# Reordering the pairs of query tiles in a differential attention block, on one Trainium2 core

## The chip, the cores and the metric

The kernel runs on one core of one Trainium2 chip. The metric is the device time of one execution in microseconds, taken as the median of several runs; lower is better.

## What is computed

The input is one sequence of 2048 tokens with 256 channels. Cut to what matters here:

```python
qkv = hidden_states @ Wqkv_w.T + Wqkv_b          # 16 query heads, 8 key heads, D = 128
p1 = softmax(causal(q[..., 0] @ k[..., 0].T * scale))
p2 = softmax(causal(q[..., 1] @ k[..., 1].T * scale))
p = p1 - lam * p2
o = p @ v                                        # v has 2 * D = 256 columns a head
o = o * rsqrt(mean(o * o) + EPS) * subln_w * (1 - LAMBDA_INIT)
x = x + layernorm(o @ out_w.T + out_b)           # attention block
x = x + layernorm(ffn(layernorm(x)))             # feed-forward block, 256 -> 1024 -> 256
```

The attention is differential: each of 8 output heads has two softmax maps, which are combined before the product with the values. It is causal, so a query tile of 128 tokens with number i has (i + 1) * 128 keys, 128 for tile 0 and 2048 for tile 15. Everything is in float32, and TensorE gets each operand as a high and a low part of float32r.

## The kernel before, in words

After a prologue that normalises and transposes the input, the attention is a hardware loop of 4 iterations (`nc.Fori(0, GROUPS)`), one for each group of key heads, with all semaphores cleared at its end (`all_engine_barrier`, line 930). A feed-forward stage follows; it reads the results of all tiles and does not depend on the order in which they were made.

A group serves two output heads, s = 0 and s = 1, so there are 2 x 16 rows of work: a **row** is one query tile of one head, with its two maps m = 0 and m = 1. `duo_chunks` puts two rows in a **duo**: tile 15 - e of head 0 and tile e of head 1, the shorter first. A duo has always 17 key blocks of 128, cut in 5 **chunks** of at most 512 keys. Two duos (e even and the next e) are a **pair**, since their queries are projected together (`QP`), and `PAIR_ORDER` says in which order the 8 pairs come. Pair p and pair 7 - p have the same row lengths: 0 and 7 hold tiles 0, 15, 1, 14 (rows of 1 and 4 chunks), 1 and 6 tiles 2, 13, 3, 12, 2 and 5 tiles 4, 11, 5, 10, and 3 and 4 tiles 6, 9, 7, 8 (rows of 2 and 3 chunks).

`attention_steps` turns this into one list of steps, and every engine walks through the same list in order, waiting on semaphores. It is made in **halves** h, one for each map of each duo (32 halves, and 3 more that drain the pipeline); half h holds the scores of duo h // 2, map h % 2. The strings `FIRST_HALVES`, `HALVES` and `LAST_HALVES` give the interleaving within a half. The kinds of step:

- `S` (line 583, matmuls of lines 596 to 598): scores of one chunk, three matmuls in one of 4 score banks. The bank of the chunk 4 before must have been read by its exponential on ScalarE (`score_bank`, line 532). VectorE reduces each chunk to its maximum (line 801; line 796 for a row's last chunk, with the causal mask), and after a row's last chunk makes the row's negated maximum (line 805). Only then can ScalarE take the exponentials of all chunks of that row (line 702): their places in its queue are set by `exps_due` and `EXPS_AT`.
- factors: when the second map of a row has its exponentials, VectorE sums (line 865) and GpSimd makes the ratio (lines 882, 885). Then each chunk is mixed, e1 + ratio * e2: chunk 3 of a duo on VectorE (line 873), the others on GpSimd (lines 895, 898).
- `T` (line 605): transposes of a mixed chunk; ScalarE copies the high part (line 713), VectorE the low part (line 811).
- `PV` (lines 618, 620): product with the values, two matmuls a key block. After a row's last chunk ScalarE copies one half (line 722) and VectorE adds (line 822), which gives o_sum.
- `OT` (line 649) transposes o_sum, lines 729 and 828 split it, and `OP` (line 659) is the output projection, added into acc by VectorE (line 856).
- `K`, `V`, `W` and the first `QP` are projections and transposes at the head of an iteration.

The products of duo d are due three to four halves after its scores: half 3 and half 4 hold those of duo 0.

```python
EXPS_AT = {'PV': 2, 'OT': 0, 'QP': 0, 'T': 0, 'S': 2, 'OP': 2}
HALVES = ('TSSTSSPTSoQTPPPTO', 'TSTSSOSTPSoQTPPTP')
FIRST_HALVES = ('KQSKKKSVSVSSVVVVV', 'SVWSWSQSS')
LAST_HALVES = ('ToTPTToOP', 'TTOTPPTPO', 'ToTTTOoPo')
SCALAR_LAGS = {'K': 1, 'V': 1, 'QP': 0, 'OP': 0}
VECTOR_LAGS = {'PV': 1, 'T': 1, 'OT': 1, 'W': 1, 'K': 1, 'V': 1}
```

In these strings `P` takes the next `PV`, `o` the next `OT` if a row is finished, and `O` the next `OP` if one is transposed. A lag puts an engine's part of a step behind the next step's.

Of the kernel before, what the change touches and what calls it, by code (L numbers as in the profile page):

```python
# [51 lines left out]
V_USES = TILES // 2  # L52


PAIR_ORDER = (3, 7, 4, 2, 5, 1, 6, 0)


HALVES = ('TSSTSSPTSoQTPPPTO', 'TSTSSOSTPSoQTPPTP')
# [19 lines left out]
def duo_chunks(d):  # L78
# [3 lines left out]
    out = []  # L82
    e = 2 * PAIR_ORDER[d // 2] + d % 2
    for n, (i, s) in enumerate(sorted(((TILES - 1 - e, 0), (e, 1)))):
# [94 lines left out]
def build(nc, hidden, wqkv, bqkv, lq1, lk1, lq2, lk2, subln, out_w, out_b, su_ug, su_dp, ws_ug, ws_dp,  # L179
# [7 lines left out]
    with ExitStack() as whole:  # L187
# [25 lines left out]
        with ExitStack() as att:  # L213
# [271 lines left out]
            def first_q_token(u, s):  # L485
                first = 2 * PAIR_ORDER[u]
                return (TILES - 2 - first) * P if s == 0 else first * P
# [1007 lines left out]
```

## Time and profile before

| | us |
|---|---|
| runs (3) | 1506.24, 1507.68, 1508.19 |
| median | 1507.68 |
| span of the profiled execution, first to last instruction | 1506.7 |
| attention iterations, first weight transpose to the next one's | 23.6, 347.0, 670.2, 991.9 (starts) |

For the profiled execution only its span was given, no time of its own; the median of the runs is 1.0 us above that span. In the iteration that starts at 347.0 us the first scores begin at 363.2, the scores of the second pair at 402.2, the last score chunk ends at 639.9, and the last output projection ends at 665.2. The other iterations look alike. Durations in the trace: a matmul's own time includes its drain through the array, so matmuls overlap and what one costs is the distance from its start to the next one's; "idle before" counts only what is left outside.

### The profile page before, as it was taken

Reading aid. Unit: us, or ns where it says so; the run is one execution under the profiler, and the core shown is the slowest. Engines: PE = TensorE matmul, PEld = TensorE weight load, DVE = VectorE, ACT = ScalarE, POOL = GpSimd, SP = SyncE. Lnnn points to the kernel's source line nnn. Section 1 sums busy time; section 2 is a strip of 40 time slices with the busy share of each in tenths; the row PEclk is TensorE's granted clock in tenths of the full one; section 3 lists DMA queues with packets and bytes.
Section 4 is the critical chain, followed back from the end, with each engine's and each line's share of the span. In section 5 each row is a group of like instructions: output and inputs, shape, how many; then the busy total and the mean of one; then the engine's idle time right before and its main releaser. Section 6 shows DMA issues by size and latency. Waiting matters only on the chain. (4 is left out here: it accounts for less than half of the span.)

```text
span 1506.7 us, 26747 instructions
## 1 busy us (share of the span) xinstructions
PE 1404.5 (93%) x8440; PEld 1228.7 (82%) x8440; DVE 1058.8 (70%) x2630; ACT 881.2 (58%) x2489; POOL 829.8 (55%) x1316
## 2 busy tenths in 40 slices
PE   5999999988999999979999999979999999669998
PEld 4888888877888888867888888768888888547887
DVE  6677777754777787846777887647777777585654
ACT  4566666653666667645667666536666666353331
POOL 1566665650766666634666656607656566433544
PEclk9999999998999999999999999989999999979999
DMA  4000000001000000010000000010000000130000
GB/s 144 8 2 1 1 2 1 1 2 45 8 1 1 1 1 1 1 41 12 2 1 1 1 1 1 1 45 8 1 1 1 2 1 1 17 124 1 11 15 32
DMA packets 25569, 20.46 MB, mean 14 GB/s; under 512 B 8896, under 2 KB 24128, under 8 KB 25408
## 3 DMA queue, kind: packets, MB, share of 16 engines
q1 hardware_dynamic: 25408, 18.52, 4.1%
q8 instruction: 76, 1.25, 0.3%
q14 instruction: 85, 0.70, 0.1%
HBM read 16.41 MB, written 2.10 MB: 12 GB/s over the span
## 5 line engine op out<-in xcount | busy, mean ns | idle before, releaser
L702 ACT ACTIVATE e<-score_bank,negmx 128x512 f32<-128x512 f32 (+3 forms) x640 | 393.8, 625 | 78.8 <-DVE negmx L805 78.2
L898 POOL TENSOR_TENSOR e<-e 128x512 f32<-128x512 f32 (+3 forms) x256 | 284.2, 1110 | 21.4
L618 PE MATMUL turn_bank<-v_hl,pT_hi 128*128 128x512 f32 x784 | 288.4, 403 | 7.8 <-DVE pT_lo L811 7.4
L801 DVE TENSOR_REDUCE mx<-score_bank 128x1 f32<-128x512 f32 x384 | 261.2, 682 | 29.7 <-PE score_bank L598 28.8
L596 PE MATMUL score_bank<-k_hi,q_hi 128*128 128x512 f32 (+3 forms) x640 | 257.5, 402 | 10.4 <-ACT e L702 9.7
L882 POOL TENSOR_TENSOR inv_s<-s,neg_one 128x1 f32<-128x1 f32 x128 | 70.3, 549 | 309.2 <-DVE s L865 309.2
L598 PE MATMUL score_bank<-k_hi,q_lo 128*128 128x512 f32 (+3 forms) x640 | 235.7, 368 | 0.0
L597 PE MATMUL score_bank<-k_lo,q_hi 128*128 128x512 f32 (+3 forms) x640 | 235.3, 368 | 0.0
L620 PE MATMUL turn_bank<-v_hl,pT_lo 128*128 128x256 f32 x784 | 219.8, 280 | 0.0
L895 POOL TENSOR_SCALAR e<-e,ratio 128x512 f32<-128x512 f32 (+3 forms) x256 | 177.8, 694 | 12.2
L618 PEld LDWEIGHTS turn_bank<-v_hl,pT_hi 128*128 128x128 f32 x784 | 147.2, 188 | 41.3 <-DVE pT_lo L811 12.2
L796 DVE CUSTOM_DVE_ANT_0 score_bank<-score_bank,mask 128x256 f32<-128x256 f32 (+3 forms) x256 | 126.0, 492 | 54.2 <-PE score_bank L598 53.3
L620 PEld LDWEIGHTS turn_bank<-v_hl,pT_lo 128*128 128x128 f32 x784 | 148.3, 189 | 2.3
L596 PEld LDWEIGHTS score_bank<-k_hi,q_hi 128*128 128x128 f32 x640 | 121.8, 190 | 30.5 <-ACT e L702 16.8
L598 PEld LDWEIGHTS score_bank<-k_hi,q_lo 128*128 128x128 f32 x640 | 121.7, 190 | 20.1
L702 ACT ACTIVATION_READ_ACCUMULATOR e<-score_bank,negmx 128x1 f32 x640 | 131.9, 206 | 0.0
L597 PEld LDWEIGHTS score_bank<-k_lo,q_hi 128*128 128x128 f32 x640 | 122.6, 192 | 6.5
L922 POOL TENSOR_TENSOR v_hl<-e,v_hl 128x512 fp32r<-128x512 f32 x32 | 41.0, 1296 | 137.4 <-ACT v_hl L743 137.4
L713 ACT ACTIVATE pT_hi<-turn_bank 128x512 fp32r<-128x512 f32 (+2 forms) x124 | 69.7, 562 | 49.5 <-PE turn_bank L605 49.3
L811 DVE TENSOR_TENSOR pT_lo<-turn_bank,pT_hi 128x512 fp32r<-128x512 f32 (+2 forms) x124 | 78.1, 630 | 5.8 <-ACT pT_hi L713 5.2
L1461 POOL TENSOR_TENSOR h_lo<-h_f,h_hi 128x512 fp32r<-128x512 f32 x32 | 41.6, 1299 | 68.3 <-ACT h_hi L1358 68.3
L713 ACT ACTIVATE pT_hi<-sum_bank 128x512 fp32r<-128x512 f32 (+3 forms) x100 | 54.9, 549 | 40.5 <-PE sum_bank L605 39.9
(299 smaller groups left out, 3560.2 us busy)
## 6 DMA issues: line engine op xcount, KB each, us to landing
w_raw<-in_L_attn_Wqkv_w_dram SPq DMA_DIRECT2D x5, 512.0 KB, 3.5
w_raw<-in_L_attn_Wqkv_w_dram SPq DMA_DIRECT2D x10, 256.0 KB, 3.7
x_in<-_attn_hidden_states_dram SPq DMA_DIRECT2D x4, 512.0 KB, 5.7
e<-in_L_attn_out_w_dram SPq DMA_DIRECT2D x4, 512.0 KB, 4.3
out_dram<-d_out SPq DMA_DIRECT2D x16, 128.0 KB, 1.7
x_res<-_attn_hidden_states_dram SPq DMA_DIRECT2D x1, 1536.0 KB, 11.9
bv<-in_L_attn_Wqkv_b_dram SPq DMA_DIRECT2D x10, 128.0 KB, 4.1
raw<-in_L_ffn_W_up_dram SPq DMA_DIRECT2D x2, 512.0 KB, 6.2
```

The costliest lines, as they stand in the source:

```text
L596: pe.matmul(bank[:, 0:w], qh, kh, start=True, stop=False)
L597: pe.matmul(bank[:, 0:w], qh, kl, start=False, stop=False)
L598: pe.matmul(bank[:, 0:w], ql, kh, start=False, stop=True).then_inc(s_full, 1)
L618: pe.matmul(bank[:, :], pT_hi[:, q % PT_SLOTS, b * P:(b + 1) * P], v_hl[:, kt, :], start=(kt == 0), stop=False)
L620: mm = pe.matmul(bank[:, 0:HID], pT_lo[:, q % PT_SLOTS, b * P:(b + 1) * P], v_hl[:, kt, 0:HID], start=False, stop=(kt == i))
L702: act.activation(e, S[k % NS][:, 0:w], ACT.Exp, bias=negmx[:, d % 2, m, s:s + 1], accum_out=ssum[:, d % 4, s, m, c:c + 1]).then_inc(s_act, 1)
L713: act.activation(pT_hi[:, q % PT_SLOTS, 0:w], bank_for(kind, what)[:, 0:w], ACT.Copy).then_inc(t_hi, 1)
L796: dve.tensor_tensor_reduce(out=S[k % NS][:, 0:w], in0=S[k % NS][:, 0:w], in1=mask[:, BANK - w:], scale=1.0, scalar=LOWEST, op0=ALU.add, op ...
L801: dve.tensor_reduce(mx[:, d % 2, m, s, c:c + 1], S[k % NS][:, 0:w], X, ALU.max)\
L811: dve.tensor_tensor(pT_lo[:, q % PT_SLOTS, 0:w], bank_for(kind, what)[:, 0:w], pT_hi[:, q % PT_SLOTS, 0:w].bitcast(F32), ALU.subtract)\
L895: pool.tensor_scalar(b, b, ratio[:, d % 4, s:s + 1], 0.0, ALU.mult, ALU.add)\
L898: pool.tensor_tensor(a, a, b, ALU.add).then_inc(p_pool, 1)
```

## The change

The order of the pairs is changed, and nothing else. Since `duo_chunks`, `first_q_token` and `attention_steps` all read it, the lengths of rows and chunks move to other places in the list of steps, and with them the places of exponentials, factors and mixes.

```diff
-PAIR_ORDER = (3, 7, 4, 2, 5, 1, 6, 0)
+PAIR_ORDER = (0, 7, 1, 6, 2, 5, 3, 4)
```

Widths of the chunks, shorter row | longer row, in the four duos at the ends of the list:

| duo | before | after |
|---|---|---|
| 0 | 512 384 \| 512 512 256 | 128 \| 512 512 512 512 |
| 1 | 512 512 \| 512 512 128 | 256 \| 512 512 512 384 |
| 14 | 128 \| 512 512 512 512 | 512 512 \| 512 512 128 |
| 15 | 256 \| 512 512 512 384 | 512 384 \| 512 512 256 |

## Rows read from the trace of the kernel before

**Rows 1.** The page: TensorE busy, and two groups with mean ns.
```profile
PE 1404.5 (93%) x8440; PEld 1228.7 (82%) x8440; DVE 1058.8 (70%) x2630; ACT 881.2 (58%) x2489; POOL 829.8 (55%) x1316
...
L713 ACT ACTIVATE pT_hi<-turn_bank 128x512 fp32r<-128x512 f32 (+2 forms) x124 | 69.7, 562 | 49.5 <-PE turn_bank L605 49.3
L811 DVE TENSOR_TENSOR pT_lo<-turn_bank,pT_hi 128x512 fp32r<-128x512 f32 (+2 forms) x124 | 78.1, 630 | 5.8 <-ACT pT_hi L713 5.2
```

**Rows 2.** One iteration by stretch: PE, PEld, DVE, ACT, POOL busy; granted clock.
```profile
386.40:402.30 15.90, 13.55 (x68) 11.08 (x68) 11.56 (x32) 9.53 (x28) 10.89 (x16) 0.89 0.02 6
402.30:609.70 207.40, 206.91 (x1306) 184.27 (x1305) 159.90 (x408) 139.29 (x420) 131.16 (x217) 1.00 0.00 1
609.70:639.90 30.20, 29.75 (x179) 25.41 (x178) 24.11 (x59) 19.72 (x62) 18.98 (x31) 1.00 0.01 2
639.90:665.20 25.30, 20.30 (x132) 17.49 (x130) 11.51 (x28) 11.08 (x34) 13.20 (x26) 1.00 0.00 1
```

**Rows 3.** What TensorE waited for, 386.5 to 402.3: us, times, longest.
```profile
PE score_bank L596 <- ACT e L702: 2.3, 2, 2.0
```

**Rows 4.** The timeline at the longest of these waits.
```profile
386.44 0.50 PE L596 MATMUL score_bank<-k_hi,q_hi 128*128 128x512 f32 x1
...
387.85 0.42 DVE L796 CUSTOM_DVE_ANT_0 score_bank<-score_bank,mask 128x256 f32<-128x256 f32 x1
...
388.37 0.16 DVE L805 TENSOR_REDUCE negmx<-mx 128x1 f32<-128x3 f32 x1
...
388.56 0.69 ACT L702 ACTIVATE e<-score_bank,negmx 128x512 f32<-128x512 f32 x1 [1.80 <-DVE negmx L805]
...
389.23 0.68 ACT L702 ACTIVATE e<-score_bank,negmx 128x512 f32<-128x512 f32 x1
...
389.39 0.50 PE L596 MATMUL score_bank<-k_hi,q_hi 128*128 128x512 f32 x1 [1.98 <-ACT e L702]
```

**Rows 5.** TensorE alone, 391 to 402.5 us: starts, one matmul each.
```profile
391.46 0.63 PE L596 MATMUL score_bank<-k_hi,q_hi 128*128 128x512 f32 x1
...
397.69 0.40 PE L596 MATMUL score_bank<-k_hi,q_hi 128*128 128x512 f32 x1
...
398.39 0.39 PE L618 MATMUL sum_bank<-v_hl,pT_hi 128*128 128x512 f32 x1
...
400.06 0.33 PE L550 MATMUL turn_bank<-xT_hi,wq_hi 128*128 128x256 f32 x1
...
400.82 0.40 PE L618 MATMUL sum_bank<-v_hl,pT_hi 128*128 128x512 f32 x1
...
401.89 0.60 PE L605 MATMUL turn_bank<-ident,e 128*128 128x128 f32 x4
402.24 0.36 PE L596 MATMUL score_bank<-k_hi,q_hi 128*128 128x256 f32 x1
```

**Rows 6.** Granted clock at that place, in two iterations.
```profile
390.00:394.00 4.00, 4.00 (x16) 3.39 (x15) 2.66 (x9) 1.91 (x7) 3.40 (x6) 0.57 0.00 0
...
712.00:716.00 4.00, 3.54 (x23) 2.79 (x22) 3.23 (x10) 2.35 (x9) 3.71 (x6) 1.00 0.00 0
```

**Rows 7.** What TensorE waited for, 640 to 665 us.
```profile
PE sum_bank L659 <- DVE oT_lo L828: 1.3, 1, 1.3
PE turn_bank L618 <- DVE pT_lo L811: 1.1, 1, 1.1
PE turn_bank L659 <- DVE oT_lo L828: 1.0, 1, 1.0
PE proj_bank L649 <- DVE o_sum L822: 0.9, 1, 0.9
PE turn_bank L605 <- POOL e L898: 0.6, 1, 0.6
```

**Rows 8.** The timeline of the drain.
```profile
661.16 0.38 ACT L722 ACTIVATE o_half<-turn_bank 128x256 f32<-128x256 f32 x1 [1.65 <-PE turn_bank L620]
...
662.06 0.44 PE L649 MATMUL proj_bank<-ident,o_sum 128*128 128x128 f32 x2 [0.93 <-DVE o_sum L822]
```

## The prediction, made before the change was run

> **What bounds the kernel now.** First the busy times of the page: TensorE is busy for 93% of the span [rows 1]. Such a share says little by stages, so next one iteration of the loop by stretch. From 402.3 to 609.7 us TensorE is busy for 206.91 of 207.40 us, and in the following 30.2 us for 29.75 [rows 2]: these are the middle six pairs and then the last one, and they pass with next to no idle time. What is lost lies at the two ends: 2.35 of 15.9 us at the head, and 5.0 of 25.3 us after the last scores [rows 2]. Then the chain of waits, for those two places alone. At the head TensorE waits 2.3 us in two places, both for an exponential to free a score bank [rows 3]; in the drain it waits five times, for split transposes, for a row sum and once for a mix [rows 7]. So an order of pairs can cost or bring something in two places, four times each, and the 207 us between them follow TensorE's work.
>
> The work doesn't change: the same rows, chunks, masks and projections are issued in another order, so every engine's instructions are the same in kind and number. The feed-forward part and the boundary of the iterations (semaphores, weight loads) neither read the order. The question is only which waits of the ends are hidden. I followed `attention_steps` through both orders by hand for the steps at the ends.
>
> **The middle.** The duos with one short and one four-chunk row are pairs 0, 7, 1 and 6, and all four lie in the two stretches that show about 0.5 us of idle each [rows 2], with 1, 6 and 0 one after the other. In the new order the four lie together. Price 0; bounds 0 and 0.5 us an iteration. There is no idle time there to win.
>
> **The head.** Up to the last score chunk of duo 0 (386.44 in the iteration that I follow) the new order has the same work in the same steps, with projections of V and W between, and I take it as unmoved. Then:
>
> 1. *First wait, +0.8 us.* S(1,0,0) reuses the bank of the chunk four before, S(0,1,1). Before, this was a chunk of a row already exponentiated, so it ran at 386.44, and only S(1,0,1) waited, until 389.39, for the exponential of the longer row's first chunk [rows 4]. In the new order S(0,1,1) is itself the first chunk of the four-chunk row, whose maximum needs S(0,1,4). VectorE's queue ahead of that maximum (W's and QP's low parts, one plain maximum) is the same, so the negated maximum comes at 388.4 again, the exponential ends at 389.2 and S(1,0,0) starts at 389.4: 389.39 less 386.44 is 2.95 us without work, where before one chunk of 0.7 to 0.8 us ran in it and 2.2 were lost.
> 2. *The second row, +0.9.* S(1,1,0) reuses the bank of S(1,0,1), again the first chunk of a long row. From the end of S(1,0,4) the chain is: about 0.25 to VectorE, 0.71 from masked maximum to exponential (387.85 to 388.56), 0.67 for the exponential, 0.15 to TensorE [rows 4], and some 0.2 for the plain maximum still running ahead: 2.0 us. In its cover stand QP, 0.76 (400.06 to 400.82 [rows 5]), and a transpose of one block, 0.1 (0.35 for four, 401.89 to 402.24). That leaves 1.15 against the 0.3 that the second wait has now (2.3 less 2.0 [rows 3, 4]).
> 3. *Mix and copy between exponentials, +0.7.* T(0,1) now is a chunk of the long row, mixed only after four exponentials; I take 0.2 of wait, between 0 and the 0.6 of the like wait in the drain [rows 7]. ScalarE's queue puts T(0,1)'s copy (0.56 [rows 1]) between the second and third exponential of duo 1's long row. Exponentials come every 0.67 us [rows 4] and score chunks need 0.70 each (397.69 to 398.39 [rows 5]), so there is no slack to take a copy in: +0.5 at S(1,1,2), bounds 0 and 0.8.
> 4. *A row of one chunk, +1.7.* This is the largest term. Duo 0 has now a row of 128 keys, whose sum is complete with PV(0,0). The list then has S(1,1,4) and at once OT 0: two steps after its PV, where before OT 0 came ten steps later, and nearly every other OT in both lists has ten or more. In TensorE's queue all stands behind OT 0. What it waits for: after T(0,2), ScalarE's copy (0.56) goes ahead of o_half, and VectorE has, in order, T(0,2)'s low part (0.63 [rows 1]), the masked maximum of S(1,1,4) (0.71 [rows 4]) and o_sum (about 0.45, the second half of the 0.90 from copy to OT [rows 8]). With 0.25 to start and 0.1 to end that is 2.7 us from T(0,2), in which PV(0,0), one key block at 0.35 to 0.4 (1.07 for three), and S(1,1,4), three quarters of 0.70 [rows 5], are done: 1.7. Below, if ScalarE and VectorE are free, it is the bare chain, 0.90 from copy to OT (661.16 to 662.06 [rows 8]) and 0.2 before it, less 0.55: 0.5.
>
> Sum of the head: 0.8 + 0.9 + 0.7 + 1.7 = 4.1 us an iteration; low 1.3 (0.8 and the bare 0.5), high 5.3 (with 0.8 and 0.6 in point 3, and 0.5 for the middle). As a check I put the steps one behind the other: S(2,0,0) comes at about 407.4 instead of 402.24 [rows 5], of which 1.0 is work that moved ahead of it (two more key blocks of PV at 0.35 each, 1.07 for three [rows 5], two of T, one OT).
>
> *The clock.* After the wait, two score chunks take 2.07 us (389.39 to 391.46) where 1.40 is the rate elsewhere [rows 4, 5], and the granted clock of that stretch is 0.57, TensorE at 1.2 GHz for most of it; in the next iteration the same wait leaves it at 1.00 [rows 6], so even now it doesn't always fall. The drain, with five waits up to 1.3 us, stays at 1.00 [rows 2, 7]. The new order keeps the first drop and I price more drops at 0. The Trainium skill ("TensorE: Matmul & The Clock Gate", section "A second HAM failure mode: psum-queue depth-cycling") says that TensorE which idles briefly again and again while it cycles through PSUM banks can switch back and forth between its two clocks; the drain here speaks against it, the head for it. By that rule the sum would be the third rival's below.
>
> **The drain, 0.** The last row before has four chunks, now three; but three key blocks of PV only move ahead of the last scores. The waits one by one, after against before [rows 7]: OT 28 now comes two steps after its last PV (six before), behind two exponentials on ScalarE, and waits 1.3, with 0.3 more at the next PV, where before the PV behind the four exponentials waited 1.1. The mix wait of 0.6 goes, since the last row's mixes start earlier against T(15,2); but PV(15,0) now follows its T with only T(15,1) and OP 28 between, and waits 0.7. OP 29, OT 31 and OP 31 (1.3, 0.9, 1.0) stand as before. 1.3 + 0.3 + 0.7 against 1.1 + 0.6 is +0.6; each wait also costs TensorE some 0.25 outside of the idle count, and against that the shorter last row's softmax frees VectorE and ScalarE earlier. I take 0; bounds -1.7 (both old waits gone) and +1.
>
> **Sum.** 4 iterations x 4.1 = 16.4 us on a span of 1506.7: 1523.1. The median of the runs is 1.0 above that span, so 1524.1.
>
> **The rivals.**
> - *The head costs little, the drain nothing.* If ScalarE's and VectorE's queues are freer at OT 0 than I put them, and points 2 and 3 overlap, the head is 1.3 an iteration: 5.2, or 1513. For it: before, similar tight places never show in the middle; against it: there OTs have ten steps of cover.
> - *Faster.* The drain's two waits that hang on the four-chunk last row (1.1 and 0.6, 1.7 together [rows 7]) vanish with a three-chunk row and even rows. It decides if the head costs under 1.7. With the head at 0.8 (the first point alone) it is -0.9 an iteration, 3.6 in all: 1504. For it: these waits are real and hang on the order. Against: OT 28 moves right behind its PV.
> - *Clock drops in the new waits.* Points 2 and 4 make two more waits above 1 us within 16 us. The one now costs 0.67 for the two chunks shown and up to twice that over its whole stretch, so about 1.2. Two more of them an iteration are +2.4, so 4 x 6.5 = 26, or 1534.
> - *It does nothing.* All head waits fall into time that TensorE makes up later. But it is busy throughout the middle [rows 2], so nothing is made up; what is lost stays lost.
>
> **How the numbers follow.** Forecast (head 4, drain 0) 0.52; cheap head 0.17; clock drops 0.14; faster 0.10; nothing 0.07. A measurement of this kernel can tell about 0.2% (3 us) from no change. Slower takes the forecast, the clock case and most of the cheap head: 0.82; same 0.09; faster 0.09. The range leaves out the faster case and part of the clock case: 1509 (a drain 1 better under the cheap head) to 1533 (head at 5.3 and drain at 1, 4 x 6.3 = 25).
>
> **What would show it.** In the changed trace: the wait at line 596 after each iteration's first duo near 2.8 instead of 2.0, a second one near 1.1; one wait of about 1.7 at line 649 for line 822 at the head, which doesn't exist now; the middle still without idle time; the drain within 1 us of its 25.3 less 1.0 for moved work. The prediction is wrong if OT 0 doesn't wait, if the drain loses its waits without new ones, or if the clock falls more than once in a head.

## The result, and the profile after

The changed kernel takes 1513.2 us (median of 5 runs, 1512.14 to 1515.42), the kernel before 1507.68 (5 runs): a ratio of 1.0046, 95% interval 1.0031 to 1.0062. The two medians alone lie 5.5 us apart, a ratio of 1.0037. It is slower, by some 7 us by the ratio, where 16 were forecast. The span of the profiled execution went from 1506.7 to 1510.9 us.

The second iteration by stretch, as [rows 2]; the columns are the length of the stretch, the busy time and count of TensorE, its weight loads, VectorE, ScalarE and GpSimd, then the granted clock, the DMA share and GB/s:

```profile
362.60:385.50 22.90, 22.90 (x159) 21.06 (x158) 15.00 (x32) 13.15 (x30) 10.68 (x9) 1.00 0.03 7
385.50:406.80 21.30, 15.29 (x79) 12.24 (x77) 13.58 (x34) 12.09 (x37) 11.56 (x19) 0.92 0.02 7
406.80:612.00 205.20, 205.15 (x1298) 182.89 (x1295) 158.95 (x404) 138.00 (x413) 129.12 (x211) 1.00 0.01 1
```

The head, from the end of duo 0's scores to the first scores of the second pair, now takes 21.3 us and has 6.0 us of idle time in it, against 15.9 and 2.35 [rows 2]; some 0.4 of the 21.3 is the end of duo 0's last score chunk, which the stretch before leaves out. The middle is 2.2 us shorter, and its 0.5 us of idle time are gone; 1.4 of the 2.2 are steps that now stand ahead of it. What TensorE waited for in the head, as [rows 3] (total, times, longest):

```profile
PE score_bank L596 <- ACT e L702: 4.3, 3, 2.4
PE turn_bank L649 <- DVE o_sum L822: 1.6, 1, 1.6
```

and from the last score chunk on, which ends at 642.1 (640.5 to 666 us), as [rows 7]:

```profile
PE sum_bank L649 <- DVE o_sum L822: 1.1, 1, 1.1
PE turn_bank L659 <- DVE oT_lo L828: 1.0, 1, 1.0
PE turn_bank L649 <- DVE o_sum L822: 0.9, 1, 0.9
PE proj_bank L659 <- DVE oT_lo L828: 0.8, 1, 0.8
PE turn_bank L618 <- DVE pT_lo L811: 0.5, 1, 0.5
```

The timeline of TensorE in the head, each wait with the start of what comes after it:

```profile
388.47 0.58 PE L596 MATMUL score_bank<-k_hi,q_hi 128*128 128x256 f32 x1 [2.36 <-ACT e L702]
...
395.32 0.38 PE L596 MATMUL score_bank<-k_hi,q_hi 128*128 128x256 f32 x1 [1.29 <-ACT e L702]
...
398.06 0.49 PE L596 MATMUL score_bank<-k_hi,q_hi 128*128 128x512 f32 x1 [0.65 <-ACT e L702]
...
402.61 0.44 PE L649 MATMUL turn_bank<-ident,o_sum 128*128 128x128 f32 x2 [1.59 <-DVE o_sum L822]
```

These are the four waits of the prediction's points 1 to 4, in their places. So the head costs about what was forecast, and what is missing must have been given back elsewhere. To find it I made a count of **lateness**: for every step of an iteration the distance from its first matmul to the next step's, less the distance that this kind and width of step commonly has (the lower fifth of all, such as 0.69 us for an S of 512 keys and 1.39 for a PV of 512). Plain distances and lateness together make up an iteration's scores and products; the plain part is 278.1 us in both kernels. Lateness takes in whatever makes a step come late, a wait or a low clock. Mean of iterations 2 to 4, us:

| steps | before | after | difference |
|---|---|---|---|
| 2 to 24, first duo's scores, K, V, W | 0.1 | 0.25 | +0.15 |
| 25 to 45, the head | 4.8 | 8.95 | +4.2 |
| 46 to 353, the middle | 7.7 | 6.9 | -0.8 |
| 354 to 398, the last pair's scores | 2.9 | 1.45 | -1.4 |
| 399 to 425, the drain | 7.2 | 6.9 | -0.3 |
| from first weight transpose to first scores (all 4) | 15.8 | 15.0 | -0.8 |

The sum is +1.05 us an iteration, 4.2 in four, which is the difference of the spans. The +4.2 of the head would alone have been 16.8: about what was forecast, and 12.6 of it came back in sum in the other rows, 8.8 of that in the middle and the last pair's scores.

### The profile page after: what moved, and what is told of

It reads as the page before. It is cut to its first block and busy times, and to the rows that moved or that the text cites. A ratio compares the mean times of both kernels' runs of the same rounds, so it can differ in the third digit from the quotient of the medians.

```text
span 1510.9 us, 26747 instructions
## 1 busy us (share of the span) xinstructions
PE 1401.7 (93%) x8440; PEld 1228.3 (81%) x8440; DVE 1060.1 (70%) x2630; ACT 884.3 (59%) x2489; POOL 829.1 (55%) x1316
## 3 DMA queue, kind: packets, MB, share of 16 engines
q8 instruction: 76, 1.25, 0.4%
## 5 line engine op out<-in xcount | busy, mean ns | idle before, releaser
L618 PE MATMUL turn_bank<-v_hl,pT_hi 128*128 128x512 f32 x596 | 217.4, 400 | 1.9 <-DVE pT_lo L811 1.9
L895 POOL TENSOR_SCALAR e<-e,ratio 128x512 f32<-128x512 f32 (+3 forms) x256 | 176.4, 689 | 12.6
L620 PE MATMUL turn_bank<-v_hl,pT_lo 128*128 128x256 f32 x596 | 167.1, 280 | 0.0
L796 DVE CUSTOM_DVE_ANT_0 score_bank<-score_bank,mask 128x384 f32<-128x384 f32 (+3 forms) x256 | 125.9, 492 | 52.8 <-PE score_bank L598 52.8
L618 PEld LDWEIGHTS turn_bank<-v_hl,pT_hi 128*128 128x128 f32 x596 | 111.9, 188 | 26.0 <-issue 3.3
L618 PE MATMUL sum_bank<-v_hl,pT_hi 128*128 128x512 f32 x340 | 124.4, 400 | 0.0
L620 PEld LDWEIGHTS turn_bank<-v_hl,pT_lo 128*128 128x128 f32 x596 | 112.7, 189 | 1.9
L713 ACT ACTIVATE pT_hi<-turn_bank 128x512 fp32r<-128x512 f32 (+3 forms) x156 | 81.4, 522 | 40.1 <-PE turn_bank L605 39.5
L620 PE MATMUL sum_bank<-v_hl,pT_lo 128*128 128x256 f32 x340 | 95.2, 280 | 0.0
L811 DVE TENSOR_TENSOR pT_lo<-turn_bank,pT_hi 128x512 fp32r<-128x512 f32 (+3 forms) x156 | 90.2, 578 | 2.3 <-ACT pT_hi L713 2.0
```

What stands on the lines that cost most here:

```text
L618: pe.matmul(bank[:, :], pT_hi[:, q % PT_SLOTS, b * P:(b + 1) * P], v_hl[:, kt, :], start=(kt == 0), stop=False)
L620: mm = pe.matmul(bank[:, 0:HID], pT_lo[:, q % PT_SLOTS, b * P:(b + 1) * P], v_hl[:, kt, 0:HID], start=False, stop=(kt == i))
L796: dve.tensor_tensor_reduce(out=S[k % NS][:, 0:w], in0=S[k % NS][:, 0:w], in1=mask[:, BANK - w:], scale=1.0, scalar=LOWEST, op0=ALU.add, op ...
L811: dve.tensor_tensor(pT_lo[:, q % PT_SLOTS, 0:w], bank_for(kind, what)[:, 0:w], pT_hi[:, q % PT_SLOTS, 0:w].bitcast(F32), ALU.subtract)\
L895: pool.tensor_scalar(b, b, ratio[:, d % 4, s:s + 1], 0.0, ALU.mult, ALU.add)\
```

## The experiments

Each ran beside the kernel before on one chip, in three groups on three chips: after_again, long_ends, even_ends and turn_late; before_again, mix_later, even_turn and even_first4; and the three mixes_behind. Ratios are to the kernel before on the same chip. Traces hold one execution each, so the lateness and the median can differ by a few us; those of even_ends and mix_later are of their fastest runs.

**after_again**, the changed kernel for a second profile, and **before_again**, the kernel before.

> The changed kernel unaltered, for a second profile. In the first pair of traces the scores and products of an iteration took 1.5 to 2.5 us longer after the change, while the stretch from the first weight transpose to the first scores, which the order does not touch, took 14.9, 15.05, 15.3 and 14.95 us instead of 15.8, 16.2, 15.1 and 16.3. Theory A (that part is where the clock happens to stand, not the order): the ratio to the kernel before stays within 1.003 to 1.007, and in this second profile that stretch takes other values, some near 16. Theory B (the order has a lasting effect on it): the four values repeat within 0.2 us.

> The kernel before unaltered, for a second profile. In the first one the stretch from the first weight transpose to the first scores took 15.8, 16.2, 15.1 and 16.3 us, and the first head stall was followed by a fall of the clock in three of four iterations; after the change both profiles have that stretch at 14.9 to 15.5. Theory A (chance of where the clock stands): this profile has other values, with a mean that may be near 15. Theory B (bound to the list of steps): again three or four values near 16.

Measured: 1514.84 us, ratio 1.0051 (1.0037 to 1.0065), and one run of the kernel before at 1509.02. The lateness by steps came back within 0.2 us in every stretch of both. The stretch before the first scores: changed kernel 15.5, 14.85, 15.0, 15.0; kernel before 16.0, 16.2, 15.0, 16.1, the same pattern as in its first profile (15.8, 16.2, 15.1, 16.3). So it isn't chance from run to run, and theory B holds for the kernel before. For the changed kernel neither theory is right as written: single values moved by up to 0.6 us, but none is near 16, and the mean is 15.0 and 15.1. What differs is the clock. Kernel before, iterations 2 to 4, columns as above:

```profile
347.00:363.20 16.20, 15.33 (x77) 13.50 (x78) 7.33 (x12) 7.00 (x12) 0.00 (x0) 0.83 0.23 67
670.20:685.30 15.10, 14.22 (x76) 12.66 (x77) 7.64 (x15) 7.00 (x12) 0.00 (x0) 0.89 0.26 79
991.90:1008.20 16.30, 15.44 (x77) 13.60 (x78) 7.33 (x12) 7.00 (x12) 0.00 (x0) 0.82 0.22 67
```

The changed kernel at the same places:

```profile
347.50:362.60 15.10, 14.18 (x76) 12.62 (x77) 7.33 (x12) 7.00 (x12) 0.00 (x0) 0.89 0.25 72
671.40:686.70 15.30, 14.40 (x76) 12.81 (x77) 7.64 (x15) 7.01 (x12) 0.00 (x0) 0.88 0.25 74
996.30:1011.30 15.00, 14.13 (x77) 12.54 (x78) 7.24 (x12) 6.99 (x12) 0.00 (x0) 0.90 0.25 73
```

In both TensorE has just been idle for over 5 us at the boundary of iterations, and for a while it runs at 1.2 instead of 2.4 GHz; a granted clock of 0.89 over the stretch goes with 15 us, one of 0.83 with 16. In these two profiles the new order got the shorter low-clock phase, but that isn't a property of the order: turn_late below has the same order and took 15.8, 16.2, 15.0 and 15.75 us there, like the kernel before, and mixes_behind_after 16.3, 15.9, 15.8 and 15.4. Nothing in the kernel asks for it.

**long_ends**: the long head with a long end.

```diff
-PAIR_ORDER = (0, 7, 1, 6, 2, 5, 3, 4)
+PAIR_ORDER = (0, 3, 4, 2, 5, 1, 6, 7)
```

> Order (0, 3, 4, 2, 5, 1, 6, 7): the head on long rows as after the change, and a long pair (7, the mirror of 0) at the end. Theory A: head +4.1 an iteration and nothing given back at the end: 1507.7 + 16 = 1524, at least 1520. Theory B (the give-back doesn't come from the end of the list): about 1513, as after the change.

Measured: 1519.6 us, ratio 1.0077 (1.0063 to 1.009). 12 us slower than before, between the theories. Its head has the same 8.95 of lateness as the changed kernel, its middle 7.25, its last pair 2.2 and its drain 7.3: about half of what the middle and the last pair had given back is gone with this end, and so is that of the drain, and the stretch before the first scores took 15 us twice and 16 twice.

**even_ends**: the head of before with an end on even rows.

```diff
-PAIR_ORDER = (3, 7, 4, 2, 5, 1, 6, 0)
+PAIR_ORDER = (3, 7, 0, 1, 6, 2, 5, 4)
```

> Order (3, 7, 0, 1, 6, 2, 5, 4): the head of the kernel before (pairs 3, 7) with an end on even rows (5, 4). Theory A: the long rows at the head cost 4.1 us an iteration, and the end on even rows gives some of it back, about 1.5 us in the last pair and drain and up to 0.9 in the middle. Then this order is 1.5 to 2.5 us an iteration faster than the kernel before, 6 to 10 us: 1498 to 1502, with the head at its 5.0 us over the plain work. Theory B: what was given back hangs on the clock after the boundary or on long pairs standing together, not on the end. Then the time is within 2 us of 1507.7.

Measured: 1501.6 us, ratio 0.9963 (0.9949 to 0.9977), 6 us faster than before. The size is theory A's lower end, but not its place: the last pair still has 2.85 us of lateness and the drain 6.9. What fell is the middle (steps 200 to 299 from 3.1 to 2.3), the head (4.2 in all three iterations, with a granted clock of 1.00) and the stretch before the first scores (15.0 each). So "an end on even rows" is not the cause in the last pair.

**turn_late**: the changed order, with the first OT moved.

```diff
-                if to_turn:
+                if to_turn and h != 3:
```

> The changed order, but the first OT of an iteration is put 13 steps behind its PV instead of 2, all later steps keep their distances. Theory A (the fourth point of the prediction): the wait of 1.6 us at line 649 at the head vanishes and nothing takes its place: 1.75 us an iteration, so 7 us less than the changed kernel, about 1506. Rival: TensorE only runs into the next wait for exponentials sooner, since ScalarE and VectorE are behind at this place: less than 0.6 us an iteration is won, 1511 or more.

Measured: 1508.68 us, ratio 1.0013 (1.0004 to 1.0022), 6.2 us less than the changed kernel on the same chip (after_again) and 4.5 less than in its first runs. The wait at line 649 is gone from the head, whose lateness falls from 8.95 to 7.15: 1.8, the price in point 4. Of that 0.4 comes back right behind: OP 0 is now late, by a wait for line 828 that is new. The rival is refuted, and theory A right but for this part. By lateness the net gain is 1.3 us an iteration, and the stretch before the first scores took 0.6 of it back in this profile.

**mix_later**: the kernel before, with two of VectorE's mixes an iteration moved. The reason is in its timeline, in the last pair's stretch that lost 2.9 us:

```profile
614.06 1.29 POOL L898 TENSOR_TENSOR e<-e 128x512 f32<-128x512 f32 x1
...
614.17 1.73 DVE L873 SCALAR_TENSOR_TENSOR e<-e,ratio 128x512 f32<-128x512 f32 x1
...
615.21 0.48 PE L618 MATMUL turn_bank<-v_hl,pT_hi 128*128 128x512 f32 x1
...
615.82 0.69 DVE L796 CUSTOM_DVE_ANT_0 score_bank<-score_bank,mask 128x512 f32<-128x512 f32 x1
...
616.67 0.28 DVE L811 TENSOR_TENSOR pT_lo<-proj_bank,pT_hi 128x128 fp32r<-128x128 f32 x1
...
617.01 0.19 PEld L618 LDWEIGHTS turn_bank<-v_hl,pT_hi 128*128 128x128 f32 x1 [0.48 <-DVE pT_lo L811]
617.01 0.50 PE L618 MATMUL turn_bank<-v_hl,pT_hi 128*128 128x512 f32 x1
```

VectorE's mix, of duo 13, starts 0.11 us after GpSimd's add and takes 1.73 us, where others take 0.74. That fits a mix that moves only once the add has ended (614.06 + 1.29 = 615.35, and 0.55 later it is done). The masked maximum and the low part stand behind it in VectorE's queue, and TensorE's next PV begins 1.80 us after the last (615.21 to 617.01) instead of 1.39. No idle time is counted ahead of that PV on its TensorE row, since the earlier matmul's own time covers most of it; the row of its weight load does show the wait, 0.48 us for the low part. Over the last pair's scores the weight loads waited 1.0 us for low parts in the kernel before. In the changed kernel the same duo's mix starts before GpSimd does, and GpSimd's scale pays, 1.25 instead of 0.69 us, while neither TensorE nor its weight loads show a wait in the next 5 us:

```profile
616.49 0.75 DVE L873 SCALAR_TENSOR_TENSOR e<-e,ratio 128x512 f32<-128x512 f32 x1
...
616.55 1.25 POOL L895 TENSOR_SCALAR e<-e,ratio 128x512 f32<-128x512 f32 x1
```

This agrees with the Trainium skill ("SBUF — State Buffer", section "Who interferes with whom"): VectorE with two inputs in SBUF and GpSimd reading SBUF exclude each other, the first to start keeps the shared pair of ports for its whole instruction, and the other waits.

```diff
+                        late = []
                         for kind, what, _, factors, mixes in with_lags(steps, VECTOR_LAGS):
...
+                            if kind == "T" and late:
+                                mixes = [late.pop(0)]
+                            elif any(x in ((13, 3), (14, 3)) for x in mixes):
+                                late.extend(x for x in mixes)
+                                mixes = []
                             for d, j in mixes:
```

> The kernel before, with VectorE's mix of duos 13 and 14 moved behind the next low-part subtraction in its queue; nothing else. There the mixes take 1.73 and 1.77 us instead of 0.74, beside GpSimd's adds, and the masked maximum and the low part for the next PV stand behind them; TensorE then starts PV late in the last pair. Theory A (the last pair's 1.4 us that the changed order gave back are those two blocked mixes): the time over plain work in steps 354 to 398 falls from 2.86 by 0.8 to 1.4 us an iteration, 3 to 5.5 us in all. Theory B (the time hangs on the bursts of four exponentials on ScalarE or on masked maxima of 512 columns): it stays at 2.5 or more, and the time within 2 us of before.

Measured: 1501.59 us, ratio 0.9958 (0.9945 to 0.9971), 6 us faster than before. The lateness of the last pair fell from 2.9 to 1.95, 0.9 an iteration: theory A, at its low end. The middle stayed as it was (7.7), and the 1.0 us that the last pair's weight loads waited for low parts is gone. The timeline shows why it works (this copy's lines are a few higher):

```profile
614.17 1.29 POOL L904 TENSOR_TENSOR e<-e 128x512 f32<-128x512 f32 x1
614.20 0.28 DVE L812 TENSOR_TENSOR pT_lo<-proj_bank,pT_hi 128x128 fp32r<-128x128 f32 x1
...
614.39 1.62 DVE L879 SCALAR_TENSOR_TENSOR e<-e,ratio 128x512 f32<-128x512 f32 x1
```

The mix is still blocked, 1.62 us, but the low part went ahead of it. Four times 0.9 is 3.6 us; most of the rest of the 6 us is the clock: the stretch before the first scores took 14.9, 15.1 and 14.8 us in iterations 2 to 4, and the head 4.2 in two of three.

**mixes_behind_before**, **mixes_behind_after**: the same for all mixes, in either order.

```diff
+                        late = []
                         for kind, what, _, factors, mixes in with_lags(steps, VECTOR_LAGS):
...
+                            if kind == "T":
+                                mixes, late = late, []
+                            else:
+                                late.extend(x for x in mixes if x[1] in DVE_MIXES)
+                                mixes = []
                             for d, j in mixes:
```

> The order before, with every mix of VectorE moved behind the low-part subtraction of the next T in its queue. Theory A (blocked mixes ahead of low parts cost the middle and the last pair of this order): the last pair's lateness falls from 2.9 to about 2.0 us an iteration as in mix_later, and that of steps 200 to 299 from 3.1 to about 2.4, since three of the six blocked mixes stand there; 1.6 us an iteration, 6.5 in all, about 1501. Theory B: only duos 13 and 14 matter, as in mix_later, and the other mixes come too late for their transposes: 1502 or more.

> The changed order with the same move. The question is the distance between the two orders once no blocked mix stands ahead of a low part. Theory A (what the changed order gave back in the middle and the last pair, 2.3 us an iteration, is that fewer of its mixes are blocked at a costly place): without them only the head is left, so this kernel is 3.3 to 3.9 us an iteration slower than mixes_behind_before, 12 to 15 us, the 1524 less 1508 that was predicted. Theory B (the give-back has to do with row lengths and bursts): the distance stays at 5 to 8 us.

Measured: 1499.69 us, ratio 0.9941 (0.9928 to 0.9954) in the order before, and 1514.47 us, ratio 1.0039 (1.0026 to 1.0052) in the changed one. The order before gains 1.4 us an iteration of lateness (steps 200 to 299 from 3.1 to 2.05, the last pair from 2.9 to 2.0, against 0.6 more at step 80). The changed one gains nothing in sum: its middle and last pair fall by 0.65, its drain rises by 0.45. With no mix ahead of a low part, the two orders are 14.8 us apart instead of 7, the number of theory A. The lateness is 21.3 against 24.5 an iteration, 12.8 us in four, of which the heads are 4.7 and 9.1; the other 2 us are the stretch before the first scores, 15.35 and 15.9 on average.

That the number fits is in part luck. The stretch before the first scores was 0.8 us an iteration in favour of the changed order and is now 0.5 against it, which alone makes 5 of the 10 us by which the spans of the profiled executions moved apart (4.2 to 14.2). What the theory is about, the changed order's lead in the middle and the last pair, went only from 2.2 to 1.55 us an iteration:

| lateness, mean of iterations 2 to 4, us | before | after | mixes_behind_before | mixes_behind_after |
|---|---|---|---|---|
| steps 46 to 99 | 1.55 | 1.2 | 2.15 | 1.1 |
| steps 200 to 299 | 3.1 | 2.55 | 2.05 | 2.35 |
| the last pair's scores | 2.85 | 1.45 | 1.95 | 1.3 |

In the last two rows, where the order before has its blocked mixes, the lead shrinks from 1.95 to 0.35, as the theory has it; but the same move widens it in the first row from 0.35 to 1.05, mostly by the new wait at step 80 in the order before. The durations in the other traces agree for steps 200 to 299: the mixes of duos 8, 9 and 10 take 1.75 to 1.8 us there in the kernel before and in long_ends, and the lateness is 3.1 in both; in the changed kernel only that of duo 10 does (2.55), in even_ends none of them (2.3).

**mixes_behind_even**, and the drain of even_ends: **even_turn**, **even_first4**.

```diff
-LAST_HALVES = ('ToTPTToOP', 'TTOTPPTPO', 'ToTTTOoPo')
+LAST_HALVES = ('TTPTToOP', 'TTOTPPTPO', 'ToTTTOoPo')
```

even_turn has this in the order of even_ends; even_first4 has it with the order (4, 7, 0, 1, 6, 2, 5, 3).

> Order (3, 7, 0, 1, 6, 2, 5, 4) with the same move, as a candidate for the fastest. Theory A: even_ends still has 2.85 us of lateness in its last pair, with OT waiting up to 1.0; two of its blocked mixes stand at 590 and 608 us, so about 0.9 us an iteration is won: 1498. Rival: its lateness there is the OT behind o_sum, which a mix that comes later only pushes: within 1.5 us of 1501.6.

> Order (3, 7, 0, 1, 6, 2, 5, 4), and in the drain the OT that came two steps behind its PV comes five steps behind. Theory A: its wait of 1.1 us goes, and since the next PV then waits up to 0.5 longer for its low part, 0.6 to 1 us an iteration is won against even_ends: 2 to 4 us, 1498 to 1500. Rival: the wait only moves to the next PV, whose low part is behind the exponentials in ScalarE's queue: within 1 us of even_ends, 1501 to 1502.

> As even_turn, with pairs 3 and 4 exchanged: (4, 7, 0, 1, 6, 2, 5, 3). Duo 0 then ends in a chunk of 128 keys instead of 256, duo 1 has rows 6 and 9, and the drain ends on rows 7 and 8. Theory A (the head stall is the chain from the last score chunk of duo 0 through the masked maximum): it shortens by the 0.13 us between masked maxima of 256 and 128 columns and little else, so within 2 us of even_turn. Rival: the drain with its last chunk of 128 gains another 0.5 an iteration: 2 us less.

Measured: mixes_behind_even 1500.27 us, ratio 0.9947 (0.9935 to 0.9959); 1.3 us less than even_ends by the medians, but 2.4 by the ratios, which compare within one chip each, so the time doesn't decide between theory and rival. Its last pair's lateness does fall, from 2.85 to 1.24, but its drain has 0.5, its steps 46 to 99 have 0.6 and its head 0.5 more. even_turn 1501.17 us, ratio 0.9962 (0.9951 to 0.9973), the same as even_ends: the rival is right. In the drain of even_ends OT 28 waited 1.1 us for o_sum; moved, it waits no more, and the next PV does, 2.0 us in two waits in the drain of even_turn where even_ends has one of 0.5:

```profile
PE turn_bank L618 <- DVE pT_lo L811: 2.0, 2, 1.5
```

even_first4 1512.45 us, ratio 1.0032 (1.0021 to 1.0044). Both of its theories were wrong: it is 11 us slower than even_turn. Its drain has 9.1 us of lateness in two of three iterations against 7.1, with waits for line 811 of up to 1.9 (2.2 in sum in one drain), and its head 4.5, 5.3 and 6.6. Exchanging pairs 3 and 4, with nearly the same row lengths, costs more than the change studied here. Why was not followed further.

## Why the prediction came out wrong

**The head: right in its sum, with luck, since point 1 was wrong.** By points, in lateness of iteration 2, before and after: the first wait (S(0,1,4) to S(1,0,0) or S(1,0,1)) with the low clock behind it 4.2 and 4.1; S(1,1,0) and T(0,1) to S(1,1,1) 0.8 and 2.0; S(1,1,2) 0 and 1.0; OT 0 0 and 1.9. Point 1 forecast +0.8 and got nothing: from the end of S(0,1,4) to S(1,0,0) TensorE stands for 2.5 us (388.47 less 385.25, less 0.7 for the chunk) and not 3.0. VectorE is less behind than I took it to be: the masked maximum starts 0.7 us after the chunk's end (386.67), where in the order before it started 1.7 after (387.85). Points 2 and 3 forecast +0.9 and +0.7 and are +1.2 and +1.0, and point 4 has 0.2 more than its 1.7; together that is the 0.8 that point 1 lacks. The waits of points 2 and 3 are 1.29, 0.1 and 0.65 where 1.15, 0.2 and 0.5 were forecast. Point 4 forecast 1.7: 1.59 idle, 1.75 by distance, 1.9 with the restart, and turn_late took away 1.8. Its chain is in the timeline of the changed kernel, in the order given:

```profile
400.18 0.60 ACT L713 ACTIVATE pT_hi<-sum_bank 128x512 fp32r<-128x512 f32 x1 [1.16 <-PE sum_bank L605]
...
400.67 0.38 ACT L722 ACTIVATE o_half<-turn_bank 128x256 f32<-128x256 f32 x1
...
400.81 0.69 DVE L811 TENSOR_TENSOR pT_lo<-sum_bank,pT_hi 128x512 fp32r<-128x512 f32 x1 [0.31 <-ACT pT_hi L713]
...
401.42 0.56 DVE L796 CUSTOM_DVE_ANT_0 score_bank<-score_bank,mask 128x384 f32<-128x384 f32 x1
...
402.14 0.41 DVE L822 TENSOR_TENSOR o_sum<-turn_bank,o_half 128x256 f32<-128x256 f32 x1
```

The sum was forecast at 4.1 us an iteration and is 4.2 in the table. A little of it is the clock, which now falls once in every iteration's head and before did so in three of four, at 0.85 us each.

**The middle: this step of the prediction failed.** "Price 0; bounds 0 and 0.5 us an iteration. There is no idle time there to win." Measured: -0.8 in the middle and -1.4 in the last pair's scores, which I had counted to it, 2.2 us an iteration or 9 in all, with the other sign. The prediction took TensorE's busy share for its pace: 206.91 of 207.40 us busy [rows 2], and yet 7.7 us of lateness in it. Waits that end within the modelled drain of the last matmul leave no idle time, but they show in the distances of starts. Their cause is shown in part. In the last pair, moving two mixes of the order before brought back 0.9 of the 1.4 us (mix_later); moving all of them closed 1.6 us of the lead at the places of the blocked mixes and opened 0.9 elsewhere, so that 1.55 of the 2.2 us still stood. Which mixes are blocked and what stands behind them changes with the order, and GpSimd's and VectorE's queues have to be laid beside each other to see it. What the rest of the lead comes from is open.

**The drain: right in size.** "I take 0": -0.3. OT 28 waits 1.1 (1.3 forecast), the wait of 0.6 for a mix is gone, and PV(15,0) waits 0.5 (0.7 forecast). OP 29 waits 0.8 instead of the 1.3 that I left standing.

**The boundary: left out.** I wrote that the boundary of the iterations does not read the order. Its work doesn't, its clock did: -0.8 us an iteration, repeated in the second profiles, 3 of the 12 us that the forecast was too high. It doesn't follow the order: with the first OT moved (turn_late) or the mixes moved (mixes_behind_after) the same order took 0.6 and 0.8 us more there than the changed kernel. What sets it is open. Since TensorE's phases of low clock also end at other places in kernels that differ only in VectorE's queue (mix_later), any of these edits may win or lose up to 1 us an iteration (4 us of the time, against differences of 5 to 7 us).

**The rivals.** Cheap head had the time (1513), but its mechanism is refuted: the head costs its full 4.2. More clock drops did not come: the clock falls once in a head. The faster case and that of no effect were refuted by the time.

## What to carry to other kernels

Before a stretch is priced at nothing because its bounding engine shows no idle time, compare the distances between starts with the plain ones, and look at the waits of the weight loads; waits shorter than a matmul's drain add up to microseconds that a reordering can give or take. Where VectorE and GpSimd both work on SBUF, a two-input operation of one can wait for the whole of the other's, so put what another engine waits for ahead of it in the queue. Orders that look alike (3 and 4 exchanged) can differ by 11 us, so candidates are best run. The lowest time here (mixes_behind_before, 0.9941) kept the order and moved one kind of operation in one queue; mixes_behind_even (0.9947) can't be told from it.

## What the runs showed of the hardware

- A VectorE operation with both big inputs in SBUF took 1.73 us instead of 0.74 when it started 0.11 us after a GpSimd add of 1.29 us, and GpSimd's scale took 1.25 instead of 0.69 when VectorE had started 0.06 us ahead. In both cases the duration is that of an operation which stands until the first has ended and then has 0.55 us to go.
- After 5.1 to 5.6 us without work at the iteration boundary the stretch of projections ran at a granted clock of 0.83 or 0.89, 16.2 or 15.1 us. The pattern over the four iterations came back in a second profile of the same kernel (16, 16, 15, 16) and changed with edits that do not touch the stretch.
- A stretch in which TensorE counted as busy for 206.91 of 207.40 us held 7.7 us of steps that came late.
